# Token loads, the first group of heads and the first attention scores, reordered in a two-layer kernel

## The chip, the cores and the metric

One Trainium2 chip, one core of it. The metric is device microseconds (us) of one launch of the whole program; lower is better. The engines are PE (matrix products), DVE and ACT (element work, reductions, activations), POOL (element work) and SP, which here only issues DMA.

## The reference, cut to what matters

Sixteen sequences of 128 tokens with 512 features (`x`) and a context of the same shape go through two layers. All is float32.

```python
x = x + mlstm(layernorm(x), ctx, ctx, Wi, bi, Wf, bf, ln_scale)   # 2 streams as 16 blocks, 16 heads of 32
x = x + ffn_of_experts(layernorm(x), ...)                         # 8 experts, 2 of them per token, and a shared one
x = x + cross_attention(layernorm(x), ctx, ...)                   # 16 heads of 128, keys and queries rms-normed
x = x + ternary_linear(layernorm(x), weight, bias)

# mlstm, per block of the sequence and head h:
log_D = tril(cumsum(log_sigmoid(f))_row - cumsum(...)_col + i);  m = max(log_D)
C = (q_h @ k_h.T) / sqrt(32) * exp(log_D - m)
h = (C / (max(|sum(C)|, exp(-m)) + 1e-6)) @ v_h;  out = groupnorm(h) * ln_scale

# cross attention:
q = rms_norm(x @ q_w + q_b);  k = rms_norm(ctx @ ki_w + ki_b);  v = ctx @ vi_w + vi_b
out = softmax(q_h @ k_h.T / sqrt(128)) @ v_h;  x = x + concat(out) @ o_w + o_b
```

## The kernel before, in words

The tokens are held as G = 4 groups of GB = 4 sequences. A float32 product is done in three passes over operands that are split into a "lead" (rounded) and a "trail" (the remainder), so one unit of 128 x 512 outputs over 512 inputs is C = 4 chunks of 3 matmuls, 12 in all (`three_passes`, L118; its matmuls show as L120, L121, L122). The program is a row of phases, one block each; at the end of a block all engines meet, and the next block begins after that (L86 in the waits).

Engines work through their own lists in order and wait for one another through counting semaphores. The lists are written out by hand, step by step; a `wait_ge` holds everything behind it on that engine.

**Phase values** (`values_and_gates`, L185) turns the context into columns (`turn`), splits it, and computes 52 units of attention's value heads, u = 0 to 51. Units 0 to 3 are done chunk by chunk at the start. SP issues, in this order: context groups and the first value weights, then `load_ctx(2)`, `load_x(0)`, `load_ctx(3)`, `load_x(1..3)` (1024 KB each), then six loads of the gates' weights (`Wi`, `Wf`, L270) and their biases, then, in a loop over u, the stores of finished units (`store_four`, L280 on, one store for four units, 1024 KB), the next value weights and others. Two buffers `out` take finished units in turn, so ACT's `keep_even` and DVE's `keep_odd` of unit 8 wait (`room`) until the first store has landed. ACT also makes the leads of the turned context (`turn_lead`), DVE the trails (`turn_trail`). From unit STATS on DVE takes the row statistics of x, at unit NORMS the weights of the gates are split, and at the units GATES[g] the normalised x of a group is turned, the gates are computed, and their running sums and maxima follow over the next 12 units. At the end of the phase ACT and DVE split the first key weight (`A.weight_lead`, `A.weight_trail`).

**Phase heads** (`heads_and_keys`, L694) runs the recurrent heads and, between them, attention's keys. A body goes over PER = 16 heads, n = 0 to 15, of one group. For each head POOL masks a tile of running maxima (`mask`, AHEAD = 5 heads ahead, from a ring of 4 loads of two heads each), ACT takes four exponentials (`exp`, two heads ahead) and DVE multiplies with the scores (`decayed`, one head ahead). For each four heads PE computes the next four scores and the outputs (`scores`, L1305, and `outputs`, L1317, at n % 4 == 2), DVE copies the outputs out of the bank (`gather`), PE transposes them (`turn_heads`, L1324, at n % 4 == 3) and ACT copies them to `hraw` (`quad`, L1024). The key units (64 of them, 12 matmuls each) are woven in, one per step: `keys_at` runs key unit n - LAG of the group, with LAG = 8, and in the first group the eight units of `OPENING`. Each key unit needs a weight lead and a weight trail where a new weight column begins; the leads of the first 8 are made by POOL (`early_lead`), all others by ACT (`weight_lead`); DVE makes all trails, and ACT and DVE keep the key, its square and the sum of squares (`keep_key`, `add_square`). After the last body eight key units are left; beside them DVE and ACT normalise the heads of the last group, add them to x and take the statistics that the next phase begins with.

**Phase queries** (`queries`, L2335) computes 64 units of queries. Late in it, PE computes the scores of attention's heads 0 and 1 of group 0 (`SCORED`), ACT their exponentials, and DVE divides head 0 (`DIVIDED`). **Phase attention** (`attend_and_last`, L2811) then runs 64 steps of score, softmax, transpose of the probabilities (`turn_prob`, L3187), product with the values (`mix`, L3198) and output projection. Its first steps scale the keys of heads 2 and 3 (`keys`), score them (`score`, L3179) and transpose head 0's probabilities.

## Time and profile before

| | us |
|---|---|
| runs of the kernel before | 1374.69, 1381.75, 1386.12 (median 1381.75) |
| the profiled execution | 1377.97 |
| its span, first to last instruction | 1376.3 |

| engine | busy us | share of the span |
|---|---|---|
| PE | 1294.3 | 94% |
| DVE | 830.6 | 60% |
| ACT | 748.7 | 54% |
| POOL | 389.6 | 28% |

The times come from executions without a profile; the profile is one further execution. Stretches in the text count from the span's start. The phase values ends at 196, heads at 488, queries at 1010.

### The profile page before, as it was taken

The numbers are of one execution on the slowest core, as the hardware profiler recorded it, in microseconds if no ns is written. First come the engines' busy times: TensorE is split into PE (matmuls) and PEld (weight loads), VectorE is DVE, ScalarE is ACT, GpSimd is POOL, SyncE is SP. The second block draws the span as 40 slices with busy tenths as digits, with TensorE's granted clock in tenths as the row PEclk, the third lists the DMA queues.
The fourth block names the chain that finished last, engine by engine and source line by source line (L and its number), as shares of the span: only waits on it lengthen the run. The fifth ranks groups of instructions, "written<-read, shape, count | busy, mean of one in ns | idle before, by whom it ended". The sixth has DMA issues, their size and how long they took to land. (4 is left out here: it accounts for less than half of the span.)

```text
span 1376.3 us, 24515 instructions
## 1 busy us (share of the span) xinstructions
PE 1294.3 (94%) x7390; PEld 1071.6 (78%) x7391; DVE 830.6 (60%) x1598; ACT 748.7 (54%) x1848; POOL 389.6 (28%) x365
## 2 busy tenths in 40 slices
PE   7899976799999999999998989999989999999998
PEld 6688865577777768778886778888878888888887
DVE  3545545477766765354444467635477777777965
ACT  4334445587988542155446545544577555555551
POOL 0111024363828104469631054036001000000041
PEclk9999997899999899999999999999999999999999
DMA  8657895878687476475657887374565555555403
GB/s 290 235 214 254 298 301 191 283 216 282 210 273 245 161 215 261 154 242 175 206 145 248 288 262 233 98 247 148 192 190 159 166 159 168 159 163 155 125 33 123
DMA packets 168183, 280.99 MB, mean 204 GB/s; under 512 B 29920, under 2 KB 58336, under 8 KB 167840
## 3 DMA queue, kind: packets, MB, share of 16 engines
q1 hardware_dynamic: 142288, 224.44, 51.7%
q0 software_dynamic: 8672, 29.37, 6.5%
q10 hardware_dynamic: 17136, 26.09, 5.1%
q8 instruction: 47, 0.77, 0.2%
q14 instruction: 40, 0.33, 0.1%
HBM read 171.04 MB, written 108.80 MB: 203 GB/s over the span
## 5 line engine op out<-in xcount | busy, mean ns | idle before, releaser
L120 PE MATMUL banks<-of_shared_split,key_lead 128*128 128x512 f32 x256 | 108.8, 425 | 25.5 <-DVE key_trail L1405 21.5
L2986 ACT ACTIVATE prob<-banks,attend_row,rq 128x128 f32<-128x128 f32 x248 | 110.6, 470 | 0.0
L2999 ACT ACTIVATE attend_ol<-banks,of_attend_vbias 128x512 fp32r<-128x512 f32 x64 | 44.2, 691 | 116.3 <-PE banks L3198 116.3
L120 PE MATMUL banks<-wo,attend_ol 128*128 (+1 forms) x256 | 106.2, 415 | 0.0
L122 PE MATMUL banks<-of_shared_split,key_trail 128*128 128x512 f32 x256 | 103.7, 405 | 0.0
L121 PE MATMUL banks<-of_shared_split,key_lead 128*128 128x512 f32 x256 | 103.3, 403 | 0.0
L120 PE MATMUL banks<-queries_rows_split,queries_wl 128*128 128x512 f32 x256 | 100.9, 394 | 0.0
L122 PE MATMUL banks<-wo,attend_ot 128*128 (+1 forms) x256 | 100.7, 393 | 0.0
L121 PE MATMUL banks<-wo,attend_ol 128*128 (+1 forms) x256 | 99.9, 390 | 0.0
L122 PE MATMUL banks<-queries_rows_split,queries_wt 128*128 128x512 f32 x256 | 99.8, 390 | 0.0
L121 PE MATMUL banks<-queries_rows_split,queries_wl 128*128 128x512 f32 x256 | 99.7, 390 | 0.0
L2968 POOL TENSOR_TENSOR x_kept<-x_kept,attend_tern_bias 128x512 f32<-128x512 f32 x12 | 15.5, 1294 | 282.9 <-ACT of_attend_raw L3025 281.0
L2636 DVE TENSOR_TENSOR queries_total<-queries_total,queries_sq 128x512 f32<-128x512 f32 x60 | 44.6, 745 | 75.7 <-ACT queries_sq L2549 75.7
L120 PE MATMUL banks<-of_shared_split,of_ctx_lead 128*128 128x512 f32 x208 | 84.4, 406 | 5.0 <-DVE of_ctx_trail L476 4.8
L2545 ACT ACTIVATE queries_head<-banks,queries_bias 128x512 f32<-128x512 f32 x64 | 44.1, 689 | 81.2 <-PE banks L122 74.4
L1015 ACT ACTIVATE heads_dec<-mlstm_gmax,mlstm_nat 128x128 f32<-128x128 f32 x264 | 83.6, 390 | 8.4 <-POOL mlstm_gmax L914 4.8
L1208 DVE TENSOR_TENSOR heads_total<-heads_total,heads_ksq 128x512 f32<-128x512 f32 x60 | 51.5, 858 | 59.6 <-ACT heads_ksq L1066 59.3
L120 PEld LDWEIGHTS banks<-of_shared_split,key_lead 128*128 128x128 f32 x256 | 50.3, 197 | 43.0 <-DVE key_trail L1405 25.9
L122 PE MATMUL banks<-of_shared_split,of_ctx_trail 128*128 128x512 f32 x208 | 82.9, 399 | 0.0
L121 PE MATMUL banks<-of_shared_split,of_ctx_lead 128*128 128x512 f32 x208 | 82.6, 397 | 0.0
L3087 DVE TENSOR_TENSOR x_kept<-x_kept,banks 128x512 f32 (+1 forms) x64 | 44.0, 688 | 60.7 <-PE banks L122 60.0
L3179 PEld LDWEIGHTS banks<-attend_kn,q_ahead 128*128 128x128 f32 x496 | 66.1, 195 | 6.2 <-issue 1.9
(399 smaller groups left out, 3558.4 us busy)
## 6 DMA issues: line engine op xcount, KB each, us to landing
mlstm_gmax<-running_max SPq DMA_DIRECT2D x36, 512.0 KB, 5.7
k_heads<-heads_key ACTq DMA_DIRECT2D x64, 256.0 KB, 4.5
q_heads<-queries_head SPq DMA_DIRECT2D x64, 256.0 KB, 2.9
q_ahead<-q_heads SPq DMA_DIRECT2D x64, 256.0 KB, 4.1
of_attend_k<-k_heads SPq DMA_DIRECT2D x60, 256.0 KB, 4.0
of_attend_v<-v_heads SPq DMA_DIRECT2D x60, 256.0 KB, 3.3
key_raw<-in_L_xattn_ki_w SPq DMA_DIRECT2D x20, 512.0 KB, 5.8
sorted_rows<-of_shared_split SPq DMA_DIRECT2D x2, 5120.0 KB, 28.7
```

The source lines that it names most:

```text
L120: nc.tensor.matmul(out, lead_l, lead_r, start=first, stop=False)
L121: nc.tensor.matmul(out, lead_l, trail_r, start=False, stop=False)
L122: return nc.tensor.matmul(out, trail_l, lead_r, start=False, stop=last)
L1015: ins = nc.scalar.activation(dec[:, n % 2, b], gmax[:, h // 2 % 4, h % 2 * N + b * S:h % 2 * N + (b + 1) * S], ACT.Exp, scale=-1.0, bias=M ...
L1208: nc.vector.tensor_tensor(t, t, ksq[:, m % 2, :], ALU.add).then_inc(total_done, 1)
L2545: nc.scalar.activation(head[:, u % HEADS_RING, :], ps[:, u % 4, :], ACT.Identity, bias=bias[:, h:h + 1]).then_inc(head_done, 1)
L2636: nc.vector.tensor_tensor(t, t, sq[:, u % 2, :], ALU.add).then_inc(total_done, 1)
L2968: nc.gpsimd.tensor_tensor(K.x[:, b, :], K.x[:, b, :], tern_bias[:], ALU.add).then_inc(tern_bias_done, 1)
L2986: ins = nc.scalar.activation(prob[:, j % 2, b, :], ps[:, j % 2, b * S:(b + 1) * S], ACT.Exp, bias=row[:, j % 2, 1, b:b + 1], scale=rq[:, b ...
L2999: nc.scalar.activation(ol[:, par, j, :], ps[:, 4 + j % 2, :], ACT.Identity, bias=vbias[:, bass.ds(quad_of(it) * 4 + j, 1)]).then_inc(ol_do ...
L3087: nc.vector.tensor_tensor(xb, xb, ps[:, 6 + b % 2, :], ALU.add).then_inc(acc_done, 1)
L3179: ins = nc.tensor.matmul(ps[:, j % 2, s], q[:, j, s], kn[:, j % 2, s], start=True, stop=True)
```

## The change

In the values phase the loads of x leave the beginning of SP's list and stand in its loop, at units 4, 5, 7 and 9, each but the first behind a wait for PE's product. Statistics, gate weights and gates move by two units, and the gates of the groups stand 6 units apart rather than 7. The splits of two key weights, not one, are made at the end.

In the heads phase LAG is 4 rather than 8, and the first group runs 12 key units rather than 8. POOL's leads are gone; ACT makes them. `quad` moves from ACT to DVE, behind `decayed` at n % 4 == 0. SP loads the context of the group after next at n = 12 to 15 rather than 8 to 11, the split context of the second group at n = 4 to 11 rather than 8 to 15, and that of the later groups in one run at n = 10 rather than in two at n = 14 and 15. Four key units are left after the last body, and the list beside them is reordered.

At the end of the queries phase PE scores heads 2 and 3 (`next_scores`, into the banks of the last query units) and transposes head 0's probabilities; DVE scales the two keys at units 60 and 61. The attention phase leaves these out of its first steps.

```diff
-        STATS, NORMS = 6, 14
-        GATES = [18 + (UNITS - 13 - 18) // 3 * g for g in range(G)]
+        STATS, NORMS = 8, 16
+        GATES = [20 + (UNITS - 13 - 20) // 3 * g for g in range(G)]
+        TOKENS = {4: 0, 5: 1, 7: 2, 9: 3}
             sp.wait_ge(turned, C)
             load_ctx(2)
-            load_x(0)
             sp.wait_ge(turned, 2 * C)
             load_ctx(3)
-            for g in range(1, G):
-                load_x(g)
...
                 if u % 4 == 0 and u:
                     store_four(u // 4 - 1)
+                if u in TOKENS:
+                    if u > 4:
+                        sp.wait_ge(product, u - 1)
+                    load_x(TOKENS[u])
...
                         A.weight_lead(act, 0, 0)
+                        A.weight_lead(act, 1, 0)
...
             A.weight_trail(dve, 0, 0)
+            A.weight_trail(dve, 1, 1)
...
-    LAG = 8
-    OPENING = (0, 1, 2, 3, 6, 9, 12, 15)
+    LAG = 4
+    OPENING = (0, 1, 2, 3, 5, 6, 8, 9, 11, 12, 14, 15)
...
-                    if g + 2 < G and n == LAG:
+                    if g + 2 < G and n == PER - GB:
                         sp.wait_ge(ctx1_done, g + 2)
...
-                    if first and n >= LAG:
+                    if first and LAG <= n < LAG + 2 * C:
                         A.load_split(sp, 1, n - LAG)
-                    if not first and not last and n >= PER - 2:
-                        if n == PER - 2:
-                            sp.wait_ge(product, CLOSES[g - 1] + 1)
-                        for part in range(C):
-                            A.load_split(sp, g + 1, (n - PER + 2) * C + part)
+                    if not first and not last and n == PER - 2 - LAG:
+                        sp.wait_ge(product, CLOSES[g - 1] + 1)
+                        for part in range(2 * C):
+                            A.load_split(sp, g + 1, part)
...
                 for n in range(PER):
-                    if first and n + 1 in OPENING:
-                        early_lead(0, OPENING.index(n + 1))
                     mask(g, n + AHEAD)
...
-            def quad(g, c):
-                act.wait_ge(quad_turned, g * QUADS + c + 1)
...
+            def quad(g, c):
+                dve.wait_ge(quad_turned, g * QUADS + c + 1)
+                if c == 0 and g:
+                    dve.wait_ge(norm_done, FIRST + g - 1)
+                nc.vector.tensor_copy(hraw[:, half(g), :, 4 * c:4 * c + 4, :].rearrange("p b j e -> p b (j e)"),
+                                      ps[:, 0, :].rearrange("p (b w) -> p b w", b=GB)).then_inc(h_done, 1)
...
                     decayed(g, n + 1, first)
+                    if n % 4 == 0:
+                        if n:
+                            quad(g, n // 4 - 1)
+                        elif not first:
+                            quad(g - 1, QUADS - 1)
...
-            finish(PER - LAG)
+            quad(last, QUADS - 1)
             divisor(last)
             close(last, 0)
             close(last, 1)
-            for m in range(1, 4):
-                finish(PER - LAG + m)
+            finish(PER - LAG)
+            finish(PER - LAG + 1)
...
-        KN, SCORED, PEAKS, EXPS, DIVIDED = {54: 0, 55: 1}, {57: 0, 58: 1}, {58: 0, 59: 1}, {59: 0, 62: 1}, {62: 0}
+        KN, SCORED, PEAKS, EXPS, DIVIDED = {54: 0, 55: 1, 60: 2, 61: 3}, {57: 0, 58: 1}, {58: 0, 59: 1}, {59: 0, 62: 1}, {62: 0}
...
+            def next_scores(j):
+                pe.wait_ge(kn_done, j + 1)
+                pe.wait_ge(sq_done, len(UNITS) - 5 + j)
+                pe.wait_ge(head_done, len(UNITS) - 5 + j)
+                for b in range(GB):
+                    cols = slice(b * S, (b + 1) * S)
+                    ins = nc.tensor.matmul(ps[:, j - 2, cols], q_ahead[:, j, cols], kn[:, j % 2, cols], start=True, stop=True)
+                ins.then_inc(scores, 1)
+
+            next_scores(2)
+            pe.wait_ge(prob_done, 1)
+            pe.wait_ge(sq_done, len(UNITS) - 1)
+            for b in range(GB):
+                nc.tensor.transpose(ps[:, 2, b * S:(b + 1) * S], prob[:, 0, b, :], K.ident[:])
+            next_scores(3)
...
-            keys(0, 2)
             cols = slice((G - 1) * GB, B)
...
                 for j in range(4):
-                    ahead(it, par, j, 2, lambda i, p, k: score(i, k))
-                    turn_prob(it, j)
+                    if not (isinstance(it, int) and it * 4 + j < 2):
+                        ahead(it, par, j, 2, lambda i, p, k: score(i, k))
+                    if not (isinstance(it, int) and it * 4 + j == 0):
+                        turn_prob(it, j)
```

## Rows read from the trace of the kernel before

**Rows 1.** The page, part 1: busy us, share of the span, instructions.

```profile
PE 1294.3 (94%) x7390; PEld 1071.6 (78%) x7391; DVE 830.6 (60%) x1598; ACT 748.7 (54%) x1848; POOL 389.6 (28%) x365
```

**Rows 2.** Windows of heads: length, busy PE PEld DVE ACT POOL, clock, DMA share, GB/s.

```profile
196.20:264.00 67.80, 44.83 (x402) 34.51 (x403) 30.55 (x47) 33.24 (x91) 33.74 (x38) 0.80 0.70 225
264.00:445.00 181.00, 167.80 (x1394) 133.37 (x1393) 128.06 (x187) 150.83 (x343) 100.39 (x95) 1.00 0.78 251
445.00:488.30 43.30, 39.32 (x164) 31.25 (x163) 30.20 (x63) 21.91 (x38) 6.10 (x5) 0.88 0.39 130
```

**Rows 3.** SP in order of time, 22 to 45: start, us, line, DMA issued.

```profile
22.83 2.03 SPq L252 DMA_DIRECT2D x_kept<-in_x  x3
24.90 12.92 SPq L270 DMA_DIRECT2D values_w_gate<-in_L_xattn_Wi  x3
37.87 4.09 SPq L270 DMA_DIRECT2D values_w_gate<-in_L_xattn_Wf  x3
...
43.08 0.40 SPq L284 DMA_DIRECT2D v_heads<-of_ffn_raw  x1
```

**Rows 4.** ACT in order of time, 39 to 50; in brackets idle before, releaser.

```profile
48.35 0.60 ACT L397 ACTIVATE of_ffn_raw<-banks 128x512 f32<-128x512 f32 x1 [7.65 <-DMA v_heads<-of_ffn_raw]
```

**Rows 5.** PE in order of time, 54 to 57.

```profile
56.23 0.79 PE L120 MATMUL banks<-of_shared_split,of_ctx_lead 128*128 128x512 f32 x1 [4.57 <-DVE of_ctx_trail L476]
```

**Rows 6.** Windows again, 55 to 60.

```profile
55.00:60.00 5.00, 3.77 (x9) 3.00 (x10) 5.00 (x9) 0.87 (x2) 2.63 (x2) 0.50 0.61 231
```

**Rows 7.** PE's waits, 196 to 264: us in total, times, longest.

```profile
PE banks L120 <- DVE key_trail L1405: 18.2, 5, 6.9
PE banks L1305 <- DVE heads_cmat L1143: 2.9, 1, 2.9
...
PE banks L1324 <- DVE heads_hT L1170: 1.8, 2, 1.0
```

**Rows 8.** Groups by line, 196 to 264: busy us, mean ns; idle before.

```profile
L960 POOL TENSOR_SCALAR key_lead<-key_raw 128x512 fp32r<-128x512 f32 x7 | 10.9, 1551 | 3.3 <-PE banks L122 3.3
```

**Rows 9.** PE's waits, 264 to 445.

```profile
PE banks L1305 <- DVE heads_cmat L1143: 8.7, 7, 2.1
PE banks L120 <- DMA of_shared_split<-ctx_split: 3.8, 2, 2.9
```

**Rows 10.** Groups by line, ACT, 264 to 445.

```profile
L1024 ACT ACTIVATE heads_hraw<-banks 128x512 f32<-128x512 f32 x13 | 7.8, 599 | 22.8 <-PE banks L1324 22.8
```

**Rows 11.** Groups by line, DVE, 264 to 445.

```profile
L1170 DVE COPY heads_hT<-banks 128x512 f32<-128x512 f32 x12 | 8.2, 685 | 2.7 <-PE banks L1317 2.7
...
L1160 DVE TENSOR_REDUCE heads_cmean<-mlstm_ctx 128x16 f32<-128x512 f32 x8 | 5.1, 675 | 0.0
...
L1205 DVE COPY heads_total<-heads_ksq 128x512 f32<-128x512 f32 x3 | 1.3, 417 | 0.0
```

**Rows 12.** PE in order of time: twelve matmuls apart, and the last transposes.

```profile
434.36 0.39 PE L120 MATMUL banks<-of_shared_split,key_lead 128*128 128x512 f32 x1
...
437.11 0.39 PE L120 MATMUL banks<-of_shared_split,key_lead 128*128 128x512 f32 x1
...
444.25 0.60 PE L1324 MATMUL banks<-ident,heads_hT 128*128 128x128 f32 x4
```

**Rows 13.** DVE in order of time, 450 to 483.

```profile
451.59 0.23 DVE L1177 TENSOR_SCALAR heads_hraw<-heads_small 128x64 f32<-128x64 f32 x1
...
457.45 0.69 DVE L1405 TENSOR_TENSOR key_trail<-key_raw,key_lead 128x512 fp32r<-128x512 f32 x1 [3.27 <-ACT key_lead L1400]
...
481.97 0.38 DVE L1289 BATCH_NORM_AGGREGATE mv<-stats 128x2 f32<-128x6 f32 x4
```

**Rows 14.** PE in order of time, 1006 to 1016.

```profile
1010.23 1.83 PE L3226 MATMUL banks<-ones,queries_total 128*128 128x1 f32 x8 [2.94 <-PEq L86]
```

**Rows 15.** DVE in order of time, 1006 to 1016.

```profile
1012.10 0.16 DVE L3116 TENSOR_SCALAR rq<-banks 128x4 f32<-128x4 f32 x1 [0.69 <-PE banks L3226]
...
1014.02 0.69 DVE L3062 TENSOR_REDUCE attend_row<-banks 128x4 f32<-128x512 f32 x1 [1.09 <-PE banks L3179]
```

More of the change, by code:

```diff
@@ L1018, in exp @@
                 ins.then_inc(dec_done, 1)
-            def quad(g, c):
-                act.wait_ge(quad_turned, g * QUADS + c + 1)
-                if c == 0 and g:
-                    act.wait_ge(norm_done, FIRST + g - 1)
-                nc.scalar.activation(hraw[:, half(g), :, 4 * c:4 * c + 4, :].rearrange("p b j e -> p b (j e)"),
-                                     ps[:, 0, :].rearrange("p (b w) -> p b w", b=GB), ACT.Copy).then_inc(h_done, 1)
             def row_sums(g):
@@ L1045, in weight_lead @@
                 v = KEYS[u][2]
-                if u == FIRST_OF[v] and v >= HALF:
-                    if v == HALF:
-                        act.wait_ge(wl_done, HALF)
+                if u == FIRST_OF[v] and v >= 2:
                     act.wait_ge(product, LAST_OF[v - 2] + 1)
@@ L1073, in body @@
                 for n in range(PER):
-                    if n % 4 == 0:
-                        if n:
-                            quad(g, n // 4 - 1)
-                        elif not first:
-                            quad(g - 1, QUADS - 1)
-                    if not first or n == PER - 1:
-                        keys_at(g, n, 1, weight_lead, first)
+                    keys_at(g, n, 1, weight_lead, first)
                     exp(g, n + 2, first)
@@ L1096, in _ @@
             last = G - 1
-            quad(last, QUADS - 1)
             row_sums(last)
@@ L1102, in _ @@
                 keep_key(last, m - 1)
[L1103 removed]
+                if m == PER - LAG + 1:
                     square(last, 0)
                     square(last, 1)
[L1106 to L1107 removed]
                     act.wait_ge(early_agg, 1)
@@ L1110, in _ @@
                                          ).then_inc(early_root, 1)
+                if m == PER - LAG + 3:
+                    deviation(last)
                 if m == PER:
@@ L1195, in weight_trail @@
                 v = KEYS[u][2]
-                if v and u == FIRST_OF[v]:
+                if v >= 2 and u == FIRST_OF[v]:
                     A.weight_trail(dve, v, KEYS[u][0])
@@ L1258, in _ @@
             ins.then_inc(early_agg, 1)
-            finish(PER - LAG + 4)
             variance(last, 0)
-            finish(PER - LAG + 5)
+            finish(PER - LAG + 2)
             variance(last, 1)
-            finish(PER - LAG + 6)
-            factor(last)
             dve.wait_ge(early_root, 1)
@@ L1269, in _ @@
             nc.vector.tensor_tensor(msq[:], msq[:], K.rstd[:, early], ALU.mult).then_inc(early_ms, 1)
+            finish(PER - LAG + 3)
+            factor(last)
             dve.wait_ge(fac_done, G)
@@ L3042, in _ @@
                 dve.sem_inc(first, FIRST)
-            for opened in (kn_done, row_done, max_done):
+            dve.sem_inc(kn_done, 4)
+            for opened in (row_done, max_done):
                 dve.sem_inc(opened, OPENED)
@@ L3164, in _ @@
             pe.sem_inc(final, FIRST)
-            pe.sem_inc(scores, OPENED)
+            pe.sem_inc(scores, 4)
+            pe.sem_inc(prob_T, 1)
             def n_before(it, j):
@@ L3219, in body @@
                 for j in range(4):
-                    ahead(it, par, j, 2, lambda i, p, k: score(i, k))
-                    turn_prob(it, j)
+                    if not (isinstance(it, int) and it * 4 + j < 2):
+                        ahead(it, par, j, 2, lambda i, p, k: score(i, k))
+                    if not (isinstance(it, int) and it * 4 + j == 0):
+                        turn_prob(it, j)
                     ahead(it, par, j, -1, lambda i, p, k: mix(i, k))
```

21 lines of the change are left out of this document (6 added, 15 removed).

## The prediction

> **What bounds the kernel now.** I read the page's busy shares first: PE works 94% of the span [rows 1], so only what PE stands, or runs at half its clock, can be won. Windows by phase come second. In the heads phase the reader is to see three stretches [rows 2]: the first group, 67.8 us long with PE busy 44.8 at a granted clock of 0.80; three bodies, 181.0 long at full clock with 13 us without PE; and the end, 43.3 long at 0.88. Busy times clock gives the work at full clock: 35.9, 168 and 34.6 us. So the first group loses 31.9 us, the bodies 13, the end 8.7. Third come PE's waits, which name the releasers: in the first group DVE's key trails, 18.2 us in five waits [rows 7], which wait for POOL's leads at 1.55 us each [rows 8], on a POOL list that stands behind masks. The rest of the 31.9 is 4.7 of other waits [rows 7] and 9.0 of low clock. One more gap lies in the values phase: PE stands 4.57 us [rows 5], then runs at 0.50 [rows 6]. Its cause is two steps back: ACT stood 7.65 us for the landing of the first store of values [rows 4], and SP could issue that store only at 43.08, after three loads of x and 12.92 us of issuing `Wi`, where the like-sized `Wf` took 4.09 [rows 3].
>
> **The change part by part.** The sum is made against the profiled execution, 1377.97, which is 3.8 under the median of the runs shown.
>
> *Values.* Without x ahead of them the six gate loads should issue like `Wf`: from 22.8 on, 4.1 + 4.1 and 1.1 for the biases, so the first store goes out at 32.1 instead of 43.1. It took 5.3 from issue to landing [rows 3, 4]: 37.4, against 40.7, where ACT began to wait (48.35 less 7.65). The gap of 4.57 goes, and with it the half-clock stretch (half of 3.77, 1.9): 6.5. If `Wi` still takes 12.92, the store lands at 46.2 and the wait shrinks by 2.2 only. I take the first, because the loads of x are what stands ahead of the slow issue. The four token loads now wait on SP for PE's products; behind them stand the next value weights and the second store. That store cannot go before unit 7 ends, so the waits cost it nothing, but four transfers of 1024 KB are then in line ahead of it: one after another at 5.3 they would land some 4 us too late, and the gap would only have moved. Both ends: 6.5 to 0 gained. Gates 6 units apart ask for the buffer of normalised x one unit sooner (2.75, [rows 12]); I take nothing, as PE has banks ahead, and 2.75 as the bound. The second key split adds one trail, 0.69 [rows 13], on DVE at the phase's end; its lead lies beside PE's last unit. Sum: -5.8.
>
> *First group.* Twelve key units instead of eight add 4 x 2.75 = 11.0 of PE work [rows 12]: 46.9 at full clock. What is still lost? The first two leads are ready from the phase before, so two of the five long waits can only come later: I take 3.4 for the third unit, half of the longest wait of this kind (6.9, [rows 7]; bounds 0 and 6.9). In each of four rounds PE waits for `gather`, 0.9 as before (1.8 in two, [rows 7]), and once or twice for `quad` and the trail behind it on DVE (0.69 + 0.69, [rows 11, 13]) where no unit stands between: 5. Low clock, 9.0 for 22.9 of waits before, gives 0.39 for each us: 3. Together 11, bounds 5 and 20. The group is then 57.9 long instead of 67.8: -9.9, with four units more behind it.
>
> *Bodies.* `quad` leaves ACT: 13 copies of 0.60 and 22.8 us in which ACT stood for PE's transposes [rows 10], ahead of the exponentials that `decayed` needs. PE waited 8.7 us for `decayed` [rows 9]; I take half of it back, 4 (bounds 8.7 and, below nothing, 3.8 more, if the split context, now eight loads in one run behind a wait on SP with the context loads after them, comes as late again as it does now [rows 9]). On DVE the 16 copies cost 0.69 each [rows 11] beside 128 busy of 181 [rows 2]; what covers them is the key unit that PE has in hand. Sum: -4.
>
> *End of heads.* The 11.0 us of four units are gone from it. But beside them runs DVE's chain, from the last transposes (444.25, [rows 12]) to the last statistics (482.35, [rows 13]): 38.1. Four trails and four squares less are 8 x 0.69 = 5.5; waits for ACT's leads as the 3.27 [rows 13] mostly go: 4. Left 28.6, plus about 6 to the next phase as now (488.3 less 482.35): 34.6. PE's own work there, 34.6 - 11.0 = 23.6, is less, so DVE sets the end: 43.3 - 34.6 = 8.7, taken as -9 (bounds 5 and 11). The closes now stand ahead of the next trail on DVE, so PE stands some 3 us there; it has them.
>
> *Attention.* Two scores and one transpose go into PE's idle time before the meeting of the engines (2.94, [rows 14]). The first peak then starts when DVE's root is done, 12.26 instead of 14.02 past 1000 [rows 15]: -1.8, for after that exponentials set the pace. Bounds: 0, and 4 (the 2.94 and half of the slow 1.83, [rows 14]).
>
> Sum: -5.8 - 9.9 - 4 - 9 - 1.8 = -30.5, or 1347.5; I put 1348.
>
> **The rivals.** *A, the first group keeps its length.* PE's own chain, outputs, `decayed`, exponentials, outputs, with DMA behind the masks, would fill 67.8 us without POOL's leads too, and the four units would only fill waits. For it: ACT and POOL work half of that window [rows 2]. Against: the waits named are trails, 18.2 of 22.9 [rows 7]. Without the -9.9 and the bodies' -4: 1361.
>
> *B, slower: DVE takes ACT's place as the one that stands.* `quad` blocks DVE until PE's transposes end; behind it stand, at n = 4 or so, two context sums (0.68 each) and a trail (0.69): 0.69 + 1.35 + 0.69 = 2.73 [rows 11, 13], against the 2.75 of the one unit PE has in hand. Past that point PE stands in every round. If each of 16 rounds cost a whole unit: 16 x 2.75 = 44, so 1348 + 44 = 1392. Against: DVE has 53 us free in the bodies [rows 2] and only one round per group is that full.
>
> *C, masks held up by the quads.* Copies on DVE could stop POOL's masks: 16 x 0.69 = 11, if all of it reached PE, so 1359. Against: the copy out of a bank takes 0.685 where the one out of SBUF takes 0.417 [rows 11], so it is not of the fast kind, and masks run five heads ahead. The Trainium skill (SBUF — State Buffer, Who interferes with whom) says that a copy in a two-port mode and a GpSimd instruction lock each other out for a whole instruction; by that rule the sum would be 1359 if these copies ran in such a mode, which the row speaks against.
>
> *D, moved and not gone.* The gap in values moves to the second store, the first group keeps its length and the end loses 5 only: about 1371.
>
> **How the numbers follow.** Forecast 0.67, A 0.18, B 0.05, C 0.05, D 0.05. The range goes from 1333 (losses of the first group 5, the bodies' whole 8.7, the end's 11, attention's 4: 14.6 less) to 1366 (values nothing, first group 20, bodies nothing: 18.8 more); it leaves out B, D, a part of A with no gain in values, and 0.04 below. Faster by over 1% (under some 1368, about what a measurement of this kernel tells from no change; the runs shown lie within 0.5% of their median) holds the forecast, C and most of A: 0.86. Within 1%: 0.09. Slower: 0.05.
>
> **What would show it.** Values: no PE gap near 50, the first store on SP near 32, clock 1.00 from 8 to 190. First group: no wait on trails above some 4, about 58 long, and the next body beginning with 12 units done. Bodies: PE's waits for `decayed` about halved, none for `quad`. End: some 34 long, DVE working through, PE standing. Attention: first peak within 2.5 us of the phase's start. The forecast is wrong if the first group stays above 65, if a new wait on DVE appears at every fourth head, or if PE stands for a store of values after unit 10.

## The result: 0.9% faster, where 2.2% were forecast

The changed kernel took 1365.64 us in the median of 8 runs (1362.25 to 1370.39), the kernel before 1378.22 (8 runs). The ratio is 0.991 with a 95% interval of 0.9888 to 0.9933: 12.6 us less, clear of noise and well under the forecast's 30.5. It lies 0.4 us inside the upper end of the range, 1366, and by its ratio in the case "within 1%", which was given 0.09. The profiled execution of the changed kernel, 1370.39, is the slowest of its 8; against 1377.97 before, 7.6 us are to be found in the traces.

Where they are shows best by stretches, cut at the first matmul of each phase and, within heads, at the last transposes of the first and the last group:

| stretch (us) | before | after | change | forecast |
|---|---|---|---|---|
| values | 196.10 | 203.04 | +6.9 | -5.8 |
| heads, first group | 67.23 | 55.41 | -11.8 | -9.9 |
| heads, three bodies | 180.92 | 185.44 | +4.5 | -4 |
| heads, end | 44.06 | 34.36 | -9.7 | -9 |
| experts (not touched) | 303.96 | 305.48 | +1.5 | 0 |
| queries | 217.96 | 218.94 | +1.0 | 0 |
| attention | 366.07 | 366.03 | 0.0 | -1.8 |

Two of the three terms of heads came as forecast. In these two profiles values and the bodies went the other way, 21.2 us off together; how much of that is the change, and how much one execution, the runs below tell.

**The profile after.** The page's first line, as [rows 1]: busy us, share of the span, instructions.

```profile
PE 1293.6 (95%) x7390; PEld 1069.1 (78%) x7391; DVE 841.1 (61%) x1614; ACT 743.6 (54%) x1839; POOL 381.8 (28%) x358
```

PE works as long as before. The windows of heads, as [rows 2] (length; busy PE, PEld, DVE, ACT, POOL; clock; DMA share; GB/s):

```profile
203.14:259.12 55.98, 49.78 (x449) 38.90 (x450) 33.97 (x56) 41.01 (x104) 25.71 (x33) 0.94 0.92 301
259.12:444.64 185.52, 171.56 (x1394) 135.26 (x1393) 139.73 (x201) 145.78 (x332) 100.62 (x93) 0.98 0.75 245
444.64:478.24 33.60, 27.43 (x116) 21.73 (x115) 25.47 (x56) 14.48 (x25) 5.75 (x5) 0.85 0.30 113
```

The first group holds 46.8 us of work at full clock (49.78 x 0.94), as forecast, and is 12 us shorter. The bodies have as much work as before (171.56 x 0.98 = 168), but ran at 0.98. PE's largest wait in the first group, as [rows 7] (us in total, times, longest):

```profile
PE banks L120 <- DVE key_trail L1392: 4.8, 3, 1.7
```

18.2 us of waits on trails became 4.8. And in the bodies, as [rows 9]:

```profile
PE banks L120 <- DMA of_shared_split<-ctx_split: 7.4, 2, 4.2
PE banks L120 <- DVE key_trail L1392: 3.3, 5, 1.0
PE banks L1292 <- DVE heads_cmat L1120: 2.9, 5, 1.1
```

The waits for `decayed` fell from 8.7 to 2.9, those for the split context rose from 3.8 to 7.4. Where the split was late: SP in order of time, and below it PE.

```profile
298.49 0.32 SPq L813 DMA_DIRECT2D mlstm_q<-xn_turned  x1
298.86 1.46 SPq L816 DMA_DIRECT2D mlstm_kT<-ctx_turned  x1
300.37 4.78 SPq L1382 DMA_DIRECT2D of_shared_split<-ctx_split  x8
```

```profile
312.39 0.50 PE L120 MATMUL banks<-of_shared_split,key_lead 128*128 128x512 f32 x1 [4.16 <-DMA of_shared_split<-ctx_split]
```

The eight loads stand behind the load of q, which waits for PE's scores of that step. In values, SP in order of time, as [rows 3]:

```profile
22.62 1.67 SPq L268 DMA_DIRECT2D values_w_gate<-in_L_xattn_Wi  x3
24.33 4.97 SPq L268 DMA_DIRECT2D values_w_gate<-in_L_xattn_Wf  x3
...
32.70 0.40 SPq L282 DMA_DIRECT2D v_heads<-of_ffn_raw  x1
33.14 1.67 SPq L253 DMA_DIRECT2D x_kept<-in_x  x2
34.85 1.47 SPq L289 DMA_DIRECT2D mlstm_gmax<-in_L_xattn_vi_w  x1
```

The first store went out at 32.70 (forecast 32.1), and ACT no longer waits for it there. PE stands all the same, for DVE, which waits for POOL's leads of the second value weights: DVE and then PE in order of time.

```profile
51.81 1.09 DVE L484 TENSOR_TENSOR of_shared_split<-mlstm_gmax,of_shared_split 128x512 fp32r<-128x512 f32 x1 [4.72 <-POOL of_shared_split L369]
...
54.01 0.67 DVE L479 TENSOR_TENSOR of_ctx_trail<-banks,of_ctx_lead 128x512 fp32r<-128x512 f32 x1
```

```profile
54.73 0.79 PE L120 MATMUL banks<-of_shared_split,of_ctx_lead 128*128 128x512 f32 x1 [3.86 <-DVE of_ctx_trail L479]
```

3.86 of idle time in place of 4.57 [rows 5]. This is the longest of the seven executions that have this code: in the other six the gap was 1.7 to 2.8, and in three of the old code 3.9 to 4.6. Near 135 us comes a gap that the kernel before did not have. SP, ACT and PE in order of time:

```profile
121.27 3.79 SPq L321 DMA_DIRECT2D mlstm_ctx<-in_ctx  x4
125.10 0.66 SPq L325 DMA_DIRECT2D xn_turned<-mlstm_gmax  x1
```

```profile
136.37 0.60 ACT L438 ACTIVATE mlstm_gmax<-banks 128x512 f32<-128x512 f32 x1 [4.61 <-DMA xn_turned<-mlstm_gmax]
```

```profile
137.50 0.49 PE L649 MATMUL banks<-x_lead,values_w_x 128*128 128x512 f32 x1 [2.96 <-ACT x_lead L441]
```

With gates 6 units apart the second group's store of normalised x falls on unit 30, behind that unit's burst (four context loads of 256 KB and two split stores of 1024 KB each). It landed some 11 us after its issue, and until then ACT could not use its buffer for the third group, whose gates stand at unit 32. The window 110 to 155 of the kernel before and of the changed one (columns as [rows 2]):

```profile
110.00:155.00 45.00, 45.00 (x220) 36.50 (x219) 25.30 (x39) 20.69 (x36) 5.87 (x4) 1.00 0.94 350
```

```profile
110.00:155.00 45.00, 40.47 (x187) 31.62 (x186) 24.83 (x38) 19.17 (x33) 6.03 (x4) 0.96 0.84 309
```

Idle time and half clock together (45 less 40.47 x 0.96) cost 6.1 us there.

### The profile page after: what moved, and what is told of

It is laid out like the page before. It is cut to its first block and busy times, and to the rows that moved or that the text cites. A ratio compares the mean times of both kernels' runs of the same rounds, so it can differ in the third digit from the quotient of the medians.

```text
span 1368.7 us, 24518 instructions
## 1 busy us (share of the span) xinstructions
PE 1293.6 (95%) x7390; PEld 1069.1 (78%) x7391; DVE 841.1 (61%) x1614; ACT 743.6 (54%) x1839; POOL 381.8 (28%) x358
## 5 line engine op out<-in xcount | busy, mean ns | idle before, releaser
L1192 DVE TENSOR_TENSOR heads_total<-heads_total,heads_ksq 128x512 f32<-128x512 f32 x60 | 55.7, 928 | 42.4 <-ACT heads_ksq L1050 42.4
L917 POOL TENSOR_SCALAR_AFFINE_SELECT mlstm_gmax<-mlstm_gmax 128x512 f32<-128x512 f32 x69 | 52.4, 774 | 77.8 <-DMA mlstm_gmax<-running_max 77.4
```

Source lines behind the costliest of these rows:

```text
L917: nc.gpsimd.affine_select(out=t, in_=t, compare_op=ALU.is_ge, fill=FAR, base=0, pattern=[[0, GB], [1, S]], channel_multiplier=-1).then_inc ...
L1192: nc.vector.tensor_tensor(t, t, ksq[:, m % 2, :], ALU.add).then_inc(total_done, 1)
```

## The experiments

Unless another base is named, an experiment is the changed kernel with one edit, timed beside the kernel before on the same chip. Lengths of stretches come from its profiled execution. Seven executions with the changed values phase unaltered give 198.9 to 203.0 us for it (mean 200.4), three with the old one 194.2 to 196.1 (mean 195.3): the part cost about 5 us, and the 203.0 of the profile above is the far end. Nine with the changed bodies, split loads and context loads gave 183.6 to 188.1 for the bodies (mean 186.1).

### Values

**values_back**: the old order and units.

```diff
-        STATS, NORMS = 8, 16
-        GATES = [20 + (UNITS - 13 - 20) // 3 * g for g in range(G)]
-        TOKENS = {4: 0, 5: 1, 7: 2, 9: 3}
+        STATS, NORMS = 6, 14
+        GATES = [18 + (UNITS - 13 - 18) // 3 * g for g in range(G)]
...
             load_ctx(2)
+            load_x(0)
             sp.wait_ge(turned, 2 * C)
             load_ctx(3)
+            for g in range(1, G):
+                load_x(g)
...
-                if u in TOKENS:
-                    if u > 4:
-                        sp.wait_ge(product, u - 1)
-                    load_x(TOKENS[u])
```

> The changed kernel with its values part undone (x loaded at the start of SP's list, statistics, gate weights and gates at their old units); both key splits at the phase's end stay. Theory 1 (the new order of the values phase costs time: the gap near 55 us only got another cause, and gates 6 units apart run into the burst of DMA at unit 30): the gap near 137 us goes, the one near 56 is back at about 4.6, the next phase's first matmul comes at about 197 instead of 203, and the whole is some 6 us shorter than the changed kernel, about 1359.5, ratio to before 0.986. Rival (the longer phase comes from the second key split at its end, or differs from execution to execution): the phase still ends near 203, the time stays at 1365.

1362.79 us, ratio 0.9893 (0.9874 to 0.9913). Values took 195.0, the gap near 55 is 4.73, none follows near 137. The phase says that the part costs time; the whole is too near 0.991 to say it. Both key splits are in, so they are not the loss.

**burst_later** and **store_ahead**: the burst two units later; or only the stores of normalised x issued ahead of it. (The second edit moves the store of each group; this changes the order at unit 30 and, for the third group, at unit 36.)

```diff
-                if u % 2 == 0 and 30 <= u < 30 + 2 * G:
-                    g = (u - 30) // 2
+                if u % 2 == 0 and 32 <= u < 32 + 2 * G:
+                    g = (u - 32) // 2
...
-                if u == 30:
+                if u == 32:
```

```diff
+                for g in range(G):
+                    if u == GATES[g] + 4:
+                        sp.wait_ge(xT_done, (g + 1) * C)
+                        sp.dma_start(xn_dram[...], xnT).then_inc(xT_stored, 16)
                 if u % 2 == 0 and 30 <= u < 30 + 2 * G:
...
                 for g in range(G):
                     if u == GATES[g] + 4:
-                        sp.wait_ge(xT_done, (g + 1) * C)
-                        sp.dma_start(xn_dram[...], xnT).then_inc(xT_stored, 16)
...
```

> The changed kernel with the burst of unit 30 in the values phase (four loads of the context, eight stores of its split) started two units later, so that the store of the normalised x at unit 30 goes ahead of it. Theory 1 (that store lands late because it is issued behind the burst): PE's gap of 3.0 us near 135 and the low clock behind it go, the phase is about 4 us shorter, the whole about 1361.5. Rival (gates 6 units apart are too tight by themselves): a gap of 2 us or more stays at the third group's gates, or moves to the fourth, and the time stays within 2 us of 1365.6.

> The changed kernel with the store of the normalised x issued ahead of the burst of unit 30 instead of behind it, in the same step; nothing else moves. Theory 1 (it is late for its place in the queue alone): the gap of 3.0 us at the third group's gates falls under 1, values end at 195 to 198.5, the whole is about 1362. Rival (the burst as a whole takes its bandwidth, whatever stands first): the gap stays over 2 us.

1362.61 (0.9886, 0.9856 to 0.9915) and 1359.31 (0.9862, 0.9826 to 0.9897); values 196.1 and 192.1. In store_ahead the store precedes the burst, and in PE's list from 110 to 155 one wait is left, 0.38 us (SP, then PE):

```profile
114.75 0.36 SPq L300 DMA_DIRECT2D xn_turned<-mlstm_gmax  x1
115.15 0.51 SPq L306 DMA_DIRECT2D ctx_split<-of_ctx_lead  x1
115.70 1.04 SPq L306 DMA_DIRECT2D ctx_split<-of_ctx_trail  x1
116.92 6.13 SPq L326 DMA_DIRECT2D mlstm_ctx<-in_ctx  x4
```

```profile
140.08 0.50 PE L653 MATMUL banks<-x_trail,values_w_x 128*128 128x512 f32 x1 [0.38 <-DVE x_trail L502]
```

So the place in SP's list was the cause of the second gap, all but 0.4 us of it; the spacing of 6 units by itself costs no more than that.

**raw_first** and **x_twice**: the second value weights loaded at unit 4, ahead of x; or 4 MB more to move beside x (copies of x within HBM).

```diff
+        LOADS = {u if q > 1 else 4: q for u, q in LOADS.items()}
```

```diff
...
                     load_x(TOKENS[u])
+                    g = TOKENS[u]
+                    sp.dma_start(spare[g * GB:(g + 1) * GB], a["x"][g * GB:(g + 1) * GB]).then_inc(spare_done, 16)
...
```

> The changed kernel with the load of the second value weights issued at unit 4, ahead of the first store and of the loads of x, not at unit 6 behind two of them. In the changed kernel it was issued at 34.85 us and POOL began on it at 50.27. Theory 1 (the first gap now belongs to these weights, which share the way with 3 MB of x): POOL begins at 45 or earlier, PE's gap near 54 falls from 2 to 4 us to under 1 and the half clock behind it goes, the phase is 2 to 5 us shorter, the whole about 1362. Rival (the transfers are bound as a whole up to 60 us, and what is put first only makes another late): a gap of 2 us or more comes up for a store of values or a load of x within 15 us, the time stays within 2 us.

> The changed kernel with a copy of the same 1024 KB within HBM issued behind each of the four loads of x: 4 MB more to move between units 4 and 9, of which 2 MB are issued ahead of the second value weights. Theory 1 (the transfers are bound as a whole up to 60 us, so what is late is set by the bytes): the first gap grows from 2 to 4 us to 7 or more, POOL begins on the second weights at 53 or later (50.3 in the changed kernel), the phase gets 4 us or more longer. Rival (the gap is a matter of one queue's order, the transfers have room): the gap stays under 4.5 and the phase within 2 us.

raw_first: 1365.57 (0.9894, 0.9855 to 0.9933), values 200.5. POOL began on the weights 11.5 us earlier than in the profile of the changed kernel, and a gap of 2.74 stayed, because DVE now waits for x and the turned context's trail stands behind it. POOL and DVE of raw_first:

```profile
38.77 5.88 POOL L370 TENSOR_SCALAR of_shared_split<-mlstm_gmax 128x512 fp32r<-128x512 f32 x4 [34.67 <-DMA mlstm_gmax<-in_L_xattn_vi_w]
```

```profile
46.63 1.29 DVE L137 BATCH_NORM_STATS2 stats<-x_kept 128x6 f32<-128x512 f32 x2 [6.65 <-DMA x_kept<-in_x]
```

x_twice: 1374.26 (0.9963, 0.9941 to 0.9985), values 207.8, POOL's start at 54.96, where the seven had 47.8 to 50.3, and the gap 8.38 (PE):

```profile
59.42 0.80 PE L120 MATMUL banks<-of_shared_split,of_ctx_lead 128*128 128x512 f32 x1 [8.38 <-DVE of_ctx_trail L483]
```

So up to about 60 us bytes count, and in raw_first the next late transfer took the place of the first. That the order decides nothing is not shown: three_moves, below, has the loads of raw_first, and its gap was 1.1. In the changed kernel the DMA share is 1.05 at 403 to 406 GB/s in the windows 45 to 50 and 55 to 60. The Trainium skill (DMA: Bandwidth & Descriptors, Issuing engines are not separate DMA queues) says that transfers from all issuers run on the same 16 engines and interleave. x_twice agrees that they share: with 2 MB more issued ahead of the weights POOL's start came 4.7 to 7.1 us later than in the seven. SP issues those copies itself, so that transfers of other engines share the same 16 no run here shows.

### The first group

**act_leads_before** puts ACT in POOL's place in the kernel before; **pool_leads** puts POOL back in the changed kernel.

```diff
...
-                    if first and n + 1 in OPENING:
-                        early_lead(0, OPENING.index(n + 1))
...
-                if u == FIRST_OF[v] and v >= HALF:
-                    if v == HALF:
-                        act.wait_ge(wl_done, HALF)
-                    act.wait_ge(product, LAST_OF[v - 2] + 1)
+                if u == FIRST_OF[v] and v:
+                    if v >= 2:
+                        act.wait_ge(product, LAST_OF[v - 2] + 1)
...
```

```diff
...
+                    if first and n + 1 in OPENING and OPENING.index(n + 1) < HALF:
+                        early_lead(0, OPENING.index(n + 1))
                     mask(g, n + AHEAD)
...
-                if u == FIRST_OF[v] and v >= 2:
+                if u == FIRST_OF[v] and v >= HALF:
+                    if v == HALF:
+                        act.wait_ge(wl_done, HALF)
```

> The kernel before with one thing changed: the leads of the first group's key weights are made by ACT, one step ahead of their units, instead of by POOL; still 8 units in the group, LAG 8, one split ready from the phase before. First group (heads' first matmul to the last transposes of group 0): 67.2 us before, 55.4 in the changed kernel. Theory 1 (POOL's leads behind the masks were the cause): under 58, the whole 8 to 11 us faster than before. Rival (my case A: PE's own chain with decayed and the exponentials fills the time, and only more units use it): over 64, the whole within 3 us of before.

> The changed kernel with POOL's leads back for the first group's third to eighth key weights; still 12 units in the group and LAG 4. Theory 1 (the leads on POOL are the cause of the long waits): the first group is over 64 us long again, with waits on trails of 12 us or more, the whole 9 us or more slower than the changed kernel, about 1375. Rival (12 units instead of 8 and both splits ready are what shortened it): under 59, the whole within 3 us.

| first group, us | POOL's leads | ACT's leads |
|---|---|---|
| 8 units, one split ready | 67.2 | 59.6 |
| 12 units, both splits ready | 61.3 | 55.4 |

The whole took 1372.65 (0.9946, 0.9924 to 0.9967) and 1372.84 (0.9957, 0.9938 to 0.9975). Waits on trails in the first group, of act_leads_before and of pool_leads:

```profile
PE banks L120 <- DVE key_trail L1393: 11.9, 4, 4.9
```

```profile
PE banks L120 <- DVE key_trail L1403: 6.3, 3, 3.2
```

Neither theory holds alone. ACT's leads are worth 7.6 or 5.9 us, the rest of the change in that group 5.9 or 4.2. That rest is not only the units and the second ready split: quad_act, below, has both, and with `quad` on ACT its first group took 58.6.

### The bodies

**quad_act** (the copy back on ACT), **splits_early** (the split loads one step earlier), **ctx_back** (the context loads at their old steps):

```diff
...
             def body(g, first):
                 for n in range(PER):
+                    if n % 4 == 0:
+                        if n:
+                            quad(g, n // 4 - 1)
+                        elif not first:
+                            quad(g - 1, QUADS - 1)
                     keys_at(g, n, 1, weight_lead, first)
...
```

```diff
-                    if not first and not last and n == PER - 2 - LAG:
+                    if not first and not last and n == PER - 3 - LAG:
```

```diff
-                    if g + 2 < G and n == PER - GB:
+                    if g + 2 < G and n == 8:
                         sp.wait_ge(ctx1_done, g + 2)
-                    if g + 2 < G and n >= PER - GB:
-                        load_ctx(g + 2, n - PER + GB)
+                    if g + 2 < G and 8 <= n < 8 + GB:
+                        load_ctx(g + 2, n - 8)
```

> The changed kernel with the copy of the turned heads (quad) back on ACT, ahead of the leads and exponentials at n % 4 == 0. Theory 1 (taking it off ACT is what cut PE's waits for decayed from 11.5 us to 2.9): those waits are back at 8 to 12 us, the bodies get 5 to 9 us longer, the whole about 1372. Rival (those waits fell because of the new order of the key units, and quad on DVE costs as much there): the time stays within 3 us of 1365.6.

> The changed kernel with one line changed: the eight loads of the split context stand at n = 9 of a body, not at n = 10, so ahead of the loads of q, of kT and of running maxima with their wait for the scores of that step. Theory 1 (the split comes late in the bodies because it is issued behind that wait, a unit after its buffer is free): PE's waits for the split fall from 7.9 us to under 2, the half clock behind them goes too, the bodies are about 8 us shorter, the whole about 1357.5. Rival (the queues are full in that stretch and the order on SP does not matter): the waits stay above 5 us and the time at 1364 or more.

> The changed kernel with the context of the group after next loaded at n = 8 to 11 again, not at 12 to 15. Theory 1 (the split waits for its turn on SP): one context load of 256 KB leaves the way of the split, another comes ahead of it, the waits for the split stay within 2 us of 7.9, the whole within 3 us of 1365.6. Rival (the four context loads behind the split take its bandwidth): the waits fall to about 4 as before the change, and the time by 4 to 7 us, to about 1360.

PE's waits from 255 to 455 in quad_act, then in splits_early:

```profile
PE banks L1292 <- DVE heads_cmat L1133: 10.5, 9, 1.3
PE banks L120 <- DMA of_shared_split<-ctx_split: 6.6, 2, 3.9
```

```profile
PE banks L120 <- DVE key_trail L1392: 9.3, 10, 4.0
PE banks L1292 <- DVE heads_cmat L1120: 3.1, 5, 0.9
PE banks L1311 <- DVE heads_hT L1147: 1.0, 1, 1.0
```

quad_act: 1372.98 (0.9967, 0.9945 to 0.9988), bodies 193.0; in all of heads the waits for `decayed` are 11.9, as the 11.5 before. So the move of `quad` is worth some 7 us. splits_early: 1360.26 (0.9878, 0.9851 to 0.9905), bodies 178.5, and no wait for the split is left from 255 on. SP shows why: the eight loads now go 4.7 us ahead of the load of q, as soon as the unit that frees their buffer is done.

```profile
292.60 3.89 SPq L1382 DMA_DIRECT2D of_shared_split<-ctx_split  x8
296.61 0.45 SPq L819 DMA_DIRECT2D mlstm_gmax<-running_max  x1
297.31 0.32 SPq L813 DMA_DIRECT2D mlstm_q<-xn_turned  x1
```

ctx_back: 1378.88 (1.0012, 0.9989 to 1.0034), a loss of 13 that neither theory named. In the bodies the split waits stay at 7.3 (16.7 in all of heads, less the 9.4 below), so the four context loads behind the split are not what makes it late. Of the 13, 11.6 arise in the first group, 67.0 us long: there the wait ahead of the context loads (for POOL's work on the second group's context) stands at n = 8 too and holds SP from 229 to 241, and the split loads of the second group are queued behind it.

```profile
228.62 0.36 SPq L819 DMA_DIRECT2D mlstm_gmax<-running_max  x1
241.31 0.33 SPq L809 DMA_DIRECT2D mlstm_ctx<-in_ctx  x1
241.68 0.43 SPq L1382 DMA_DIRECT2D of_shared_split<-ctx_split  x1
```

```profile
PE banks L120 <- DMA of_shared_split<-ctx_split: 9.4, 1, 9.4
```

So with the second group's split loads at n = 4 to 11, the wait and the context loads have to stand behind them.

**splits_early_before**: the same idea in the kernel before.

```diff
-                    if not first and not last and n >= PER - 2:
-                        if n == PER - 2:
+                    if not first and not last and PER - 3 <= n < PER - 1:
+                        if n == PER - 3:
...
```

> The kernel before with its split loads at n = 13 and 14 instead of 14 and 15, one step earlier. PE waited 3.8 us for them in two places. Theory 1 (the wait comes of issuing them behind the wait for scores, in the kernel before too): the waits go, the bodies are 3 to 4 us shorter, the whole 3 to 5 us faster, ratio 0.997. Rival (only the eight loads in one run of the changed kernel are late for that reason): the waits stay at 2 us or more, ratio 1.000.

1378.6 (1.0006, 0.9983 to 1.0028): no gain. The split waits fell from 3.8 to 1.8; of these 1.6 are for the second group's split, which the edit does not move, and at the two places that it moves 0.25 is left. But the waits for `decayed` rose from 11.5 to 12.9, and the bodies took 182.2, before 180.9. So the loads were late for the same reason in the kernel before, where they too were issued right behind the load of q; with `quad` on ACT an earlier split bought no time there. That the split matters only with `quad` off ACT is not shown: quad_act has it on ACT, and PE stood 6.6 us for the split.

### Attention

**attention_back** undoes the part; **attention_loads** puts the query of head 4 ahead of the key of head 5, and the roots for group 1 after four heads' loads.

```diff
...
-            next_scores(2)
...
-            next_scores(3)
...
+            keys(0, 2)
...
```

```diff
                     i, m = (it, j - 1) if j else (it - 1, 3)
+                    opening = isinstance(it, int) and it == 1
+                    if opening and j < 2:
+                        i, m = 1 - j, 0
...
-            load_rkb(1)
             for at, done in enumerate(A.q_stored):
...
                 loads(it)
+                if it == 1:
+                    load_rkb(1)
```

> The changed kernel with the queries and attention part undone. Stretch from the queries phase's first matmul to the end of the span: 584.0 us before the change, 585.0 after it. Theory 1 (the first peak comes earlier, but then the loads of the next heads' keys and queries, issued at the phase's start, set the pace, and the added work at the end of queries costs 0.7): 584.0 to 584.5, the whole within 2 us of the changed kernel. Rival (the 1.8 us that I predicted are won and the profile of one execution hides them): about 586.8, the whole 1.8 us slower.

> The changed kernel with the first loads of the attention phase in another order: the query of head 4 right behind its key, ahead of the key of head 5, and the reciprocal roots for group 1 after the first four heads' loads. In the changed kernel the score of head 4 waited for that query until 6.5 us after the phase's start. Theory 1 (these loads took what the earlier first peak had won): that score starts 5 us or less after the phase's start, and the stretch from the queries phase's start to the end is 583 to 584 us instead of 585. Rival (ACT's exponentials set the pace from the first head on): 585 within 0.7, whatever lands earlier.

attention_back: 1368.61 (0.9927, 0.9902 to 0.9951); queries and attention together 583.9. The stretch speaks for theory 1, the whole, 3.0 over the changed kernel, for the rival; one profile settles neither. Four profiles with the old attention had 583.9 to 585.9 for this stretch (mean 584.9), thirteen with the new one 582.1 to 586.4 (mean 584.0). attention_loads: 1364.84 (0.9893, 0.9855 to 0.9931); the score of head 4 starts 5.6 us after the phase's start, not 6.5, and the stretch is 582.8. The length is that of theory 1, the start is not (5 or less), and the other runs speak against it. The same thirteen executions have the changed attention in its order of loads: eight took 365.8 to 366.4 for the phase, five 363.9 to 364.4, with the same loads. What goes with the length is the clock. With the phase cut into windows of 2.5 us from its start, these are the second to the fourth of the changed kernel (366.03) and of attention_loads (363.94):

```profile
1005.17:1007.67 2.50, 2.00 (x12) 2.01 (x12) 1.59 (x3) 1.61 (x8) 0.00 (x0) 0.71 0.93 226
1007.67:1010.17 2.50, 1.32 (x6) 1.02 (x6) 2.43 (x6) 2.02 (x7) 0.00 (x0) 0.50 0.98 351
1010.17:1012.67 2.50, 2.50 (x14) 2.50 (x13) 1.39 (x5) 0.92 (x5) 0.00 (x0) 0.50 0.97 320
```

```profile
1001.86:1004.36 2.50, 2.01 (x10) 2.02 (x11) 1.74 (x3) 1.61 (x8) 0.00 (x0) 0.50 0.83 183
1004.36:1006.86 2.50, 2.50 (x19) 2.31 (x19) 1.83 (x6) 1.57 (x5) 0.00 (x0) 0.83 1.00 375
1006.86:1009.36 2.50, 1.81 (x17) 1.65 (x16) 2.39 (x6) 2.50 (x10) 0.00 (x0) 1.00 1.06 310
```

In all eight long ones the granted clock (third number from the end) is 0.63 or more in the second window and about 0.50 in the next two; in the five short ones it is 0.50 to 0.57 in the second and back at 0.74 or more in the third. The new order of loads falls in with the short ones in one execution; in best, below, the phase took 365.0 with it. Whether it helps stays open, and so does what decides when the clock falls.

### Together

two_moves is splits_early with burst_later; three_moves has raw_first as well; best is two_moves with attention_loads; two_orders is splits_early with store_ahead, so two places in SP's list and nothing else.

> The changed kernel with the split loads at n = 9 and the burst of the values phase two units later. Theory 1 (both losses are of issue order and independent): values phase 195.5 to 198 us, bodies 177 to 180, the whole about 1355, ratio to before 0.982 to 0.984. Rival (what one move wins is lost elsewhere): 1360 or more.

> The changed kernel with the split loads at n = 9, the burst two units later and the second value weights loaded first. Theory 1: 2 to 4 us below the version without the last, about 1352. Rival (the transfers are bound as a whole there): the same as without it, about 1355.

> The changed kernel with the split loads at n = 9, the burst of the values phase two units later and the new order of attention's first loads. Theory 1: the 1353.9 of the two moves less 1 to 2 us, about 1352.5, ratio to before 0.980 to 0.983. Rival (attention's loads are worth nothing): 1354, within 1 us of the two moves.

> The changed kernel with two places in SP's list changed and nothing else: the split loads at n = 9 and the store of the normalised x ahead of the burst of unit 30. Theory 1 (two losses of issue order, independent): 1359.3 less the 7 of the bodies, about 1352.5, ratio to before 0.979 to 0.983; values end at 192 to 195, bodies 177 to 181. Rival (the stores that the earlier start of heads now meets take the gain back): 1357 or more.

| kernel | median us | ratio to before |
|---|---|---|
| two_moves | 1353.86 | 0.9818 (0.9786 to 0.985) |
| three_moves | 1354.75 | 0.9824 (0.9793 to 0.9855) |
| best | 1353.0 | 0.981 (0.978 to 0.984) |
| two_orders | 1352.74 | 0.9803 (0.9776 to 0.9831) |

These four cannot be told apart by time. All beat both kernels: two_orders by 27 us against before, which is 89% of the forecast's 30.5. Its values end at 192.2, its bodies take 178.0, and PE's waits from 255 to 455 hold no split:

```profile
PE banks L120 <- DVE key_trail L1394: 9.1, 10, 4.0
PE banks L1294 <- DVE heads_cmat L1122: 2.4, 3, 1.5
```

## Why the forecast was wrong, step by step

**Values: wrong, in two steps.** "The gap of 4.57 goes" failed. The store was at fault before, but with it out of the way the second value weights were late, and with those first, x. In the trace before they stood close behind the store: POOL could begin on them only at 51.77.

```profile
51.77 5.87 POOL L367 TENSOR_SCALAR of_shared_split<-mlstm_gmax 128x512 fp32r<-128x512 f32 x4 [47.66 <-DMA mlstm_gmax<-in_L_xattn_vi_w]
```

What this step gained is part of its 6.5: idle time and half clock from 45 to 65 took 5.3 to 7.2 us in three executions of the old code (mean 6.1), and 1.7 to 6.6 in the seven (mean 4.2). The forecast bounded it by nothing gained; rival D placed what comes late next at the second store. The other step, "I take nothing" for gates 6 units apart, failed by its reasoning: it priced a buffer one unit sooner and asked what PE has in hand, but did not follow which place in SP's list the store of normalised x moves to. Moved from unit 29 to unit 30, it met the burst. From 110 to 155 idle time and half clock took 5.0 to 6.7 us in the seven, nothing in the old code, and 0.4 in store_ahead and two_orders; this is what the place cost, where 2.75 was the bound. These two ended values at 192.1 and 192.2, 8 us under the mean of the seven; the rest of the 8 lies mostly at the first gap, which in them was short, 2.0 and 1.3, and without half clock.

**First group: right.** Length 55.4 (forecast 57.9); the wait for the third unit is 1.7 (forecast 3.4, bounds 0 and 6.9). The cause was named too narrowly: act_leads_before shows that ACT's leads make 7.6 of it, and the rest of the change the rest, `quad` off ACT among it. Rival A, that the group keeps its length, is refuted.

**Bodies: the mechanism of `quad` was right, the wrong end was taken for the split.** Taking `quad` off ACT won 5.8 of the 8.7 us of waits for `decayed`, more than the 4 forecast. The lateness of the split stood in the text as a bound of 3.8 more; it came, 3.6, and with it 3.4 of low clock (171.56 less 168.1) and 2.8 more of waits on trails. What failed is setting the split at nothing: eight loads behind the wait for scores, four units before they are needed. splits_early, which moves them ahead of that wait, took the bodies to 178.5, 7.6 us under the mean of the nine. The +4.5 of the table itself rests on one profile of each kernel: act_leads_before, with the old lists in its bodies, took 187.2 for them, with a wait of 3.7 for the second group's split that the kernel before does not have. Rivals B and C did not come. DVE stood 0.8 us for the transposes in the bodies, where ACT had stood 22.8 [rows 10]; in the same windows POOL's masks took 0.798 us each, before 0.788. The Trainium skill (SBUF — State Buffer, Who interferes with whom) has a copy and a GpSimd instruction lock each other out only in a two-port mode; these copies, 0.682 us each, and the masks show no lock.

**End of heads: right.** 34.4 against 34.6, with PE standing 4.0 us once for a trail, where 3 were expected. In three of the experiments that leave this part alone it took 37.6.

**Attention: the earlier start came, the gain did not follow from it.** The first peak starts 1.25 us after the phase's start (forecast 2.0, before 3.8). What failed is "after that exponentials set the pace": in eight of the thirteen executions, the profiled one among them, the phase is as long as before (365.8 to 366.4 against 366.1), and in the profile ACT stands 1.37 us for PE's product between the first two heads' exponentials. In the other five it is 2 us shorter, which is the size of the forecast; but these differ from the eight in PE's clock, for which the forecast has no term, so the match is not a confirmation.

The rest: 1.5 in experts and 1.0 in queries. Experts took 302.7 to 307.0 in the runs of this study, whatever was changed elsewhere, so nothing is read from those 1.5. The profiled execution is 4.75 over the median of its runs; its values phase is 2.6 over the mean of the seven, and its attention phase one of the long ones, 2.0.

Two sums of the forecast are off, without effect on the outcome: the terms of the range's lower end add up to 14.9 less, not 14.6, and rival D's three losses (5.8, 9.9 and 4) lead from 1347.5 to 1367; about 1371 takes the bodies' 4 away as well.

## What to carry to other kernels

When a transfer is moved within an issuing engine's list, read that list entry by entry at its new place: what waits stand ahead of it, what burst it falls behind, and what is queued behind a wait that moves with it. The three largest surprises here (5 to 7 us in values, 7 in the bodies, 13 in ctx_back) were of this kind, and two moved issues brought the change to 27 of the 30.5 us that were forecast. Where the DMA engines are full, look in the trace before for what lands next after the late transfer: with that one out of the way, it can be the next to be waited for. Whether moving bytes to another time would end such a gap no run here tried.

## What the runs showed of the hardware that was not expected

- The same three loads of `Wi`, 32 KB each, took SP 12.92 us to issue behind 3 MB of x [rows 3] and 1.67 without it.
- At attention's start PE's granted clock falls to half in every execution. The stretch at half clock lasts 6.8 us in the profiles of the kernel before and of the changed kernel, and 3.4 in that of attention_loads (the part below 1 of each window from the phase's start, doubled, times 2.5 us). It began about 1 us later in the changed kernel than in attention_loads, and the 2 us between the two lengths of the phase go with it; of one and the same code some executions had the long stretch and some the short one.
- The same code of the values phase took 198.9 to 203.0 us; its first gap, while the DMA engines are full, was 1.7 to 3.9.
